# Reordering the opening, the ternary rows and the shared expert's first products of a fused two-layer block

## The reference, cut to what matters

```python
x = x + tanh(g_xattn[0]) * cross_attention(layernorm(x), ctx, mask, norm_w, wq, wk, wv, wo, wg)   # 16 heads, gated
x = x + tanh(g_ffn[0])   * ternary_linear(layernorm(x), weight, bias)   # rows quantised to +-127, weights to -1, 0, 1
x = x + tanh(g_xattn[1]) * sigmoid_attention(layernorm(x), ctx, ctx)    # out = V @ sigmoid(Q'K / sqrt(128)), per batch element
x = x + tanh(g_ffn[1])   * moe(layernorm(x), ...)                       # 16 experts, 4 of them per row, and 2 shared ones
```

## Time and profile before

| | |
|---|---|
| median of three runs | 1298.67 us (1297.68 to 1304.92) |
| the profiled execution | 1298.22 us, of which the span of instructions is 1296.5 us |
| PE busy | 1215.9 us (94% of the span) |
| DVE, ACT, POOL busy | 668.9, 575.7, 430.9 us |
| mean granted clock of PE | 0.981 of full |

### The profile page before, as it was taken

How to read it: one execution, slowest core, us unless ns; L and a number is a source line. 1 busy time by engine, 2 the same in 40 slices (tenths; PEclk the granted TensorE clock), 3 DMA queues, 4 the chain that set the end, 5 groups by cost and what they waited for, 6 DMA issues and landing times. The chain is left out here.

```text
span 1296.5 us, 25673 instructions
## 1 busy us (share of the span) xinstructions
PE 1215.9 (94%) x7824; PEld 1026.1 (79%) x7836; DVE 668.9 (52%) x1410; ACT 575.7 (44%) x1384; POOL 430.9 (33%) x518
## 2 busy tenths in 40 slices
PE   6998999999999789988999998999999999999995
PEld 6877778788787567666777786889998989999995
DVE  6556545555545799843666644542233553424241
ACT  4555456356356668763121111543334553434342
POOL 1102211210213466340004761244434444343433
PEclk9999999999999889979999999999999999999998
DMA  9100000000000003022000221765446666645554
GB/s 334 36 17 20 18 1 20 18 1 18 17 18 1 26 26 108 8 107 100 1 1 1 91 108 59 249 165 90 76 76 148 176 150 153 146 81 135 86 140 73
DMA packets 54335, 100.36 MB, mean 77 GB/s; under 512 B 5094, under 2 KB 21990, under 8 KB 54262
## 3 DMA queue, kind: packets, MB, share of 16 engines
q0 software_dynamic: 15824, 37.76, 15.5%
q1 hardware_dynamic: 38438, 61.65, 14.7%
HBM read 72.91 MB, written 26.48 MB: 77 GB/s over the span
## 5 line engine op out<-in xcount | busy, mean ns | idle before, releaser
L1876 PE MATMUL t_H<-m_W,t_xT 128*128 128x352 f32 x1632 | 280.2, 327 | 6.4 <-DVE m_W L1954 4.9
L1876 PEld LDWEIGHTS t_H<-m_W,t_xT 128*128 128x128 f32 x1632 | 261.6, 188 | 9.6 <-DVE m_W L1954 7.5
L1844 POOL DMA_INDIRECT out_dram<-t_ys,t_sid x68 | 109.6, 1612 | 220.4 <-ACT t_ys L1905 107.3
L1921 ACT ACTIVATE t_sl<-t_H 128x352 f32<-128x352 f32 x68 | 31.6, 464 | 174.0 <-PE t_H L1876 174.0
L722 ACT ACTIVATE pr<-SC,neg 128x128 f32<-128x128 f32 x256 | 89.9, 377 | 38.2 <-DVE neg L927 38.2
L46 PE MATMUL t_Y<-m_W,t_hT 128*128 128x512 f32 (+1 forms) x207 | 87.4, 422 | 5.2 <-issue 3.1
L1999 DVE TENSOR_TENSOR t_hT<-t_TH,t_hT 128x384 fp32r<-128x384 f32 x68 | 37.8, 556 | 101.9 <-ACT t_hT L1942 100.8
L1905 ACT ACTIVATE t_ys<-t_Y,t_wcol 128x512 f32<-128x512 f32 x69 | 47.4, 687 | 93.7 <-PE t_Y L48 93.7
L1975 DVE TENSOR_TENSOR t_h<-t_H,t_sl 128x352 f32<-128x352 f32 x68 | 35.5, 523 | 102.5 <-ACT t_sl L1921 102.2
L48 PE MATMUL t_Y<-m_W,t_hT 128*128 128x512 f32 (+1 forms) x207 | 81.8, 395 | 0.0
L47 PE MATMUL t_Y<-m_W,t_hT 128*128 128x512 f32 (+1 forms) x207 | 81.5, 393 | 0.0
(11 more groups left out here) (474 smaller groups left out, 3225.6 us busy)
## 6 DMA issues: line engine op xcount, KB each, us to landing
m_raw<-in_L_ffn_w_dram SPq DMA_DIRECT2D x28, 704.0 KB, 5.2
m_raw<-in_L_ffn_w_dram SPq DMA_DIRECT2D x14, 512.0 KB, 6.5
rows_d<-before_w SPq DMA_DIRECT2D x17, 256.0 KB, 2.0
CT<-in_ctx_dram SPq DMA_DIRECT2D x8, 512.0 KB, 3.7
X<-in_x_dram SPq DMA_DIRECT2D x4, 1024.0 KB, 13.9
out_dram<-X SPq DMA_DIRECT2D x3, 1024.0 KB, 4.3
m_raw<-in_L_ffn_w_dram SPq DMA_DIRECT2D x14, 192.0 KB, 6.4
CT<-in_ctx_dram SPq DMA_DIRECT2D x8, 256.0 KB, 2.7
```

Of the source, the lines that this page charges most:

```text
L1844: pool.indirect_dma_start(out=m["out_rows"][:, :], out_offset=bass.IndirectOffsetOnAxis(ap=sid[:, b:b + 1], axis=0), in_=ys[:, b, :], in_o ...
L1876: x_ = pe.matmul(bk[b % 2][:, 0:I], xT[:, b % 2, jx, k, :], W13[:, jw, k, j, :], start=k == 0 and jx == jw, stop=k == KC - 1 and jx == 1)
```

## The change

Four edits. In the opening, `W` is taken apart into the transposition (`Wt`) and the single splits (`Ws.q.0` and so on), so that the statistics of x come ahead of DVE's splits of W.q, the first rows of x are transposed and split ahead of the splits of W.v, and the splits of W.g and W.o come later. In the last group, the rows of the ternary layer move back into the second attention. In the shared experts, POOL's subtraction is written in steps along the middle dimension. `hidden` can be asked for half of its products, and the two halves stand after tiles 6 and 7 of a group instead of both after tile 5. The plan's words are tables that order the streams; a line or two of them is shown.

```diff
-        start = ("W.k cT.0 cT.1 W.q sx.0 sx.1 sx.2 sx.3 xa.0 k.0.0 k.0.1 W.v xb.0 k.0.2 k.0.3 xd.0 nm.0 nm.1 W.g xT.0 xT.1 "
...
+        start = ("W.k cT.0 cT.1 Wt.q sx.0 sx.1 sx.2 sx.3 xa.0 Ws.q.0 Ws.q.1 k.0.0 Ws.q.2 k.0.1 xb.0 Ws.q.3 k.0.2 xd.0 nm.0 nm.1 "
...
-            "oP.3 uT.0 u.1 aS.0.2 fm.0 uT.1 fm.1 ", NG - 1)
+            "oP.3 uT.0 u.1 fm.0 ", NG - 1)
...
-                    if kind == "W":
-                        for kc in range(KC):
+                    if kind in ("W", "Ws"):
+                        for kc in s[2:] or range(KC):
...
-                    pool.tensor_tensor(lo, raw, hi.bitcast(F32), ALU.subtract).then_inc(w_lo, 1)
+                    for k in range(raw.shape[1]):
+                        i = pool.tensor_tensor(lo[:, k, :], raw[:, k, :], hi[:, k, :].bitcast(F32), ALU.subtract)
+                    i.then_inc(w_lo, 1)
...
-                def hidden(q):
+                def hidden(q, halves=(0, 1)):
...
-                    for W_, bk in ((W1[b], A[q % 2]), (W3[b], B[q % 2])):
+                    for W_, bk in [((W1[b], A[q % 2]), (W3[b], B[q % 2]))[n] for n in halves]:
...
-                    x_.then_inc(ab_fill, 1)
+                    if 1 in halves:
+                        x_.then_inc(ab_fill, 1)
...
                         logit(t // GB - 1)
-                        hidden(t // GB - 1)
+                    if t % GB == 2 and t > GB:
+                        hidden(t // GB - 1, (0,))
+                    if t % GB == 3 and t > GB:
+                        hidden(t // GB - 1, (1,))
                         logit_rows(t // GB - 1)
```

More of the change, by code:

```diff
@@ L221, in attention_and_ternary @@
         NQ, FIRST = GB * HQ, 3
-        start = ("W.k cT.0 cT.1 W.q sx.0 sx.1 sx.2 sx.3 xa.0 k.0.0 k.0.1 W.v xb.0 k.0.2 k.0.3 xd.0 nm.0 nm.1 W.g xT.0 xT.1 "
-                 "mk.0 mk.1 mk.2 mk.3 q.0.0 q.0.1 nm.2 nm.3 W.o q.0.2 q.0.3 ")
+        start = ("W.k cT.0 cT.1 Wt.q sx.0 sx.1 sx.2 sx.3 xa.0 Ws.q.0 Ws.q.1 k.0.0 Ws.q.2 k.0.1 xb.0 Ws.q.3 k.0.2 xd.0 nm.0 nm.1 "
+                 "k.0.3 Wt.v xT.0 xT.1 Ws.v.0 Ws.v.1 Ws.v.2 Ws.v.3 q.0.0 Wt.g q.0.1 mk.0 mk.1 mk.2 mk.3 nm.2 nm.3 "
+                 "Ws.g.0 Ws.g.1 Ws.g.2 Ws.g.3 q.0.2 Wt.o q.0.3 Ws.o.0 Ws.o.1 Ws.o.2 Ws.o.3 ")
         during = {0: ("sx.4 sx.5 sx.6 sx.7", "xa.1", "fq.0 xb.1", "xd.1", "ft.0 fq.1 fg.0", "ft.1 fq.2 fg.1",
@@ L249, in attention_and_ternary @@
             "bc.2 pv.5 on.2 oT.2 st.1 pT.12 v.3 Sa.7 pT.13 Sb.7 sm.14 sm.15 ra.0 "
[1 row of a table removed]
-            "oP.3 uT.0 u.1 aS.0.2 fm.0 uT.1 fm.1 ", NG - 1)
-        between = {0: "sf.-4", 1: "st.-2", 2: "sf.-3", 3: "st.-1", 5: "ra.-1", 6: "rb.-1", 7: "rd.-1 u.-2", 9: "uT.-2", 10: "u.-1",
-                   12: "fm.-2", 13: "uT.-1", 16: "fm.-1", 18: "sf.-2", 20: "sf.-1", 22: "ta.1", 24: "tb.1", 26: "tc.1", 28: "sw", 36: "ta.2", 40: "tb.2",
-                   42: "tc.2", 52: "ta.3", 56: "tb.3", 58: "tc.3"}
[1 row of a table added]
+            "oP.3 uT.0 u.1 fm.0 ", NG - 1)
+        between = {2: "uT.-3", 3: "sf.-4", 4: "fm.-3 st.-2", 6: "st.-1", 8: "ra.-1 sf.-3", 10: "rb.-1", 12: "rd.-1 u.-2", 17: "uT.-2",
+                   18: "u.-1", 20: "fm.-2", 23: "uT.-1", 25: "sf.-2", 26: "fm.-1", 28: "sw", 30: "sf.-1", 32: "ta.1", 34: "tb.1", 36: "tc.1",
+                   44: "ta.2", 48: "tb.2", 50: "tc.2", 52: "ta.3", 56: "tb.3", 58: "tc.3"}
         MS = NB * KC
@@ L519, in _ @@
                     kind, t = s[0], s[1]
-                    if kind == "W":
+                    if kind in ("W", "Wt"):
                         weight(t)
```

## The result

The changed kernel takes 1295.20 us (median of 12 runs, 1293.04 to 1297.13), the kernel before 1303.83 (12 runs, 1297.68 to 1306.27). The ratio is 0.9941 (95% interval 0.9925 to 0.9956), 7.7 us less; the medians lie 8.6 apart. Three executions of these experiments, at 1706.93, 2683.46 and 5183.80 us, were disturbed and are left out of all medians and ratios. The profiled execution takes 1293.85 against 1298.22, only 4.4 less; its span is 4.3 shorter, where 9.8 were forecast. The two differences don't agree because the kernel before has two levels of time, 1297.7 to 1299.5 (5 of the 12 runs) and 1303.3 to 1306.3 (7), and the execution that the forecast read is one of the lower level.

A forecast was written before the change was run, and what follows sets the result against it. PE is busy nearly everywhere, so gains must come from its waits and half clock. Opening +1.0, seam -6.0, POOL's steps +1.2 and products between transpositions -6.0 give -9.8: 1298.2 to 1288.4 us, range 1284 to 1292, with rivals (1) to (3) 1281 to 1296.5.

The forecast's parts named there:

- The likeliest case: Whole kernel: the forecast itself, -9.8 us to 1288.4 us, own range 1284 to 1292; chance 0.50.
- a seam of -9: Second attention: the seam's favourable bound, all 6.4 of wait and clock won without the 2 of POOL's.
- case 3: Shared experts' start: same as Rival (3); with a seam of -9 it was said to reach 1281.
- The opening: Start up to `Sa.0`: first query product at 25.8, `Sa.0` at 39.9; +1.0 us, bounds -1 and +2.5.
- The seam: Seam and second attention: moved ternary rows win at the front, little is given back; -6 us, bounds -9 and -3.
- POOL's steps: Shared experts' start: `row_scale` takes turns with POOL, low part 1.9 later; +1.2 us, bounds +1.9 and -2.3.
- The products between the transpositions: Shared experts: half chunks hide waits for low parts, last logits at full clock; -6.0 us, bounds -7 and -3.
- rival (1): Second attention: ternary rows only move, full DVE gives the front's 6.4 back; -1 for the seam, 1293.4 us; chance 0.20.
- Rival (3): Shared experts' start: POOL's steps do all they can, -2.3 instead of +1.2, 1284.9 us; chance 0.13.
- Rival (2): Shared experts: ACT undoes the interleaving, silu delays a tile's copy; -2.5 instead of -6, 1291.9 us; chance 0.12.
- Rival (4): Second attention: PE's half clock spreads, five additional spells, seam of +7.5, 1301.9 us; chance 0.05.
- The signs that the text named: Whole kernel: query product near 26, `Sa.0` near 40, `aS.2.0` near 442, `aS.8.0` about 5 earlier, logits at full clock, `row_scale` in pieces.

The follow-up runs named there:

- before_again: The kernel before, same text, run once more with nothing changed; the two such runs took 1303.52 and 1307.49 us.
- the mended kernel: The changed kernel with W.g's and W.o's splits ahead of the copies of the second, third and fourth query product: 1288.58 us, ratio 0.9880 to the kernel before.

## Why the prediction was right or wrong

**In all.** The likeliest case gave -9.8; the pair of profiles gives -4.3 and the chip, over both levels of before, -7.7. The time, 1295.2, lies in the range of all cases and outside the likeliest one's own. Faster was right, and so was the term of the products between the transpositions. The terms of the opening and of the seam were not, and that of POOL's steps was 1.4 too high. Two outer ends of the text are not what their conditions give: a seam of -9 would be -12 by the text's own terms (-6.4, -6.4 and +0.8), and case 3 with a seam of -9 is 1281.9, not 1281.

**The opening (+1.0, measured +5.1).** Its first half holds: 25.8 was forecast for the first query product, 25.63 came. Its second half failed in two places. `Sa.0` is at 41.93 instead of 39.9. Of these 2.0, 1.4 were there when the second query product started (30.35 instead of 25.8 + 1.4 + 1.75 = 28.95): the half clock of the first one, which the text left as an extra of 1.4, did come, as it does in 3 of the 11 profiles with this start. The chain of splits and transpositions behind it added the other 0.6. And the sum ended at `Sa.0`. The text knew that PE would stand still there, and wrote "this edit moves a wait", but didn't ask what the clock does behind a wait of 4: 3.1 more until the next context tile (7.97 from `Sa.0` to it instead of 4.90). Elsewhere the same text had priced such a spell at 2.0 to 2.7. The upper bound of +2.5 left it out too.

**The seam (-6, measured -1.9 from the end of the cross-attention to the first transposition).** The walk to `aS.0.3` holds (-6.8, measured -6.84). The three parts, -6.4 to `aS.2.0`, -0.4 from there to `aS.8.0` and +0.8 behind it, came out at -4.9, +2.7 and +0.2. In the first, PE waits 1.06 and 0.72 ahead of `aS.2.0` where 1.0 was counted. The failing step is in the second: "3.75 are the wait for tile 14's rows and about 2.7 the half clock behind it; both should go". They went, but the gain to `aS.4.0` was 4.9 and not 6.4. The half clock there was no loss of its own: in another execution of the kernel before (`before_again`) it is missing behind a wait of 3.59, and PE then waits 2.58 for DVE's addition to X.

```profile
456.61 0.63 PE L488 MATMUL T<-identF,fu 128*128 128x128 f32 x4 [3.59 <-DVE fu L803]
457.00 0.48 PE L46 MATMUL SC<-Wk 128*128 128x512 f32 x1
...
466.00 0.48 PE L46 MATMUL M<-Wq,Wv 128*128 128x512 f32 x1 [2.58 <-DVE X L858]
```

From `aS.2.0` to `aS.4.0` this execution takes 20.31, the one that the forecast read 20.26. Then the row work came back in the elements behind `aS.4.0`, with two new spells of half clock: 7.6, where the text's -0.4 leaves room for 6.0. The text had named each piece (11 us of DVE that no longer fit, POOL's powers ahead of element 4 with a wait of 2: measured 2.27) and booked too little for the sum of them. That is rival (1), which gave -1 here and got a chance of 0.20; it was right at this place. Its reason, that DVE is full, is only a part of it: in the mended kernel DVE is busy 30.3 of the 35.5 us of this stretch, and with 7.1 us of it and 4.6 of POOL's taken away the stretch is only 4.3 shorter.

**POOL's steps (+1.2, measured -0.2, and -3 against the two executions of the upper level).** The exchange of turns is as forecast, a step is 0.90 instead of 0.96, four of seven small steps wait for one each. Wrong is that the last two would meet the second part: `row_scale` is done at 559.25, 0.2 before it. What the text could not see is that the kernel before was lucky in the execution it showed: L97 was just ahead of POOL. Rival (3), -2.3, is near what the edit is worth where L97 falls behind, but by luck: it lets the first wait shrink, and the small steps together still take 3.8 (4.0 before). The 3 us are L97's wait.

**The products between the transpositions (-6.0, measured -5.8).** Right, and by the same route: the waits gone (but 0.97) and the last logits at full clock. The measured ratio of this edit alone, 0.9938, is that of the whole change. Rival (2) does not show but in that one wait.

**Rival (4)** is there in part: two spells of half clock in the second attention, not five. The signs that the text named came out as it said where the terms held (26 for the product, the logits at full clock with no PE wait for XT but one of 0.97, `row_scale` in pieces). Four show the forecast wrong: `Sa.0` at 41.93 and not near 40, `aS.2.0` at 447.51 and not near 442, `aS.8.0` 2.9 later than before instead of 5 earlier, and a second attention with two spells of half clock.

## What to carry to other kernels

A long wait of PE can cost more than its length: behind the 4.0 ahead of `Sa.0` the half clock took 3.1 more. So a step that is moved must be walked one stage past the wait that it causes, not up to it. But price such a spell only where PE is the limit: between `aS.2.0` and `aS.4.0` of the kernel before it cost nothing, because DVE was late as well. The cost of work that is moved into a stretch where PE and DVE are both busy 85% of the time largely came back there, in all four orders that were run. Look for the stretch where it is free, and if you write that it doesn't fit, put its length into the sum. A small operation that starts within about 0.1 us of a long one that can hold it up may give one program two levels of time: look for such pairs before trusting a single profile, and cut the long one.

## What was not expected of the hardware

One 128x4 instruction of DVE, L97, took 0.17 where it started 0.01 to 0.11 before a subtraction of POOL (three profiles), and 3.02 to 3.11 where it started 0.06 to 0.14 after it (four). L97 has one tile as its input and waits all the same. Cutting POOL's 128x1408 into four cost POOL 0.4 (3.60 instead of 3.16). In the attentions, behind the changed kernel's waits of 2.27, 2.66 and 3.97, PE's granted clock fell to 0.50, for about 3, 3 and 7 us, and behind its wait of 1.50 it didn't. But the wait alone doesn't settle it: the kernel before was at 0.50 for 5.7 us behind 3.75, and in another execution not at all behind 3.59; behind the same 1.64 or 1.65 the first query product was at half clock in 3 profiles of 11.
